# Mixture-of-experts blocks around an attention: the first phase's combines, second half's rows and one activation table stand elsewhere in the order

## The chip, the core and the metric

The kernel runs on one core of a Trainium2 chip. The core has a matrix engine (PE, with its weight loads shown as PEld), a vector engine (DVE), an activation engine (ACT), a general engine (POOL) and a queue engine (SP); each runs its own instructions in the order in which they were written, and they wait for one another on semaphores. The metric is the time of one execution on the device, in microseconds (us), as a median over runs.

## The reference

2048 tokens (4 sequences of 512) of 128 features pass three stages, each on layer-normed input and added to the stream: half of a mixture of 8 experts, a causal attention with one head, half of the same mixture again.

```python
def ffn(x):                       # x: (2048, 128)
    probs = softmax(x @ router_w.T)                  # 8 experts
    topv, topi = top_k(probs, 2)
    topv = topv / (topv.sum(-1) + 1e-9)
    cw = (one_hot(topi, 8) * topv[..., None]).sum(1)
    h = gelu(einsum('td,edh->teh', x, w1))           # h: 512 wide
    y = einsum('teh,ehd->ted', h, w2)
    return einsum('te,ted->td', cw, y)
x = x + 0.5 * ffn(layernorm(x))
x = x + attention(layernorm(x))   # softmax(QK^T / sqrt(128), causal) V
x = x + 0.5 * ffn(layernorm(x))
```

## The kernel before

**Tiling.** A tile is 128 tokens; the tokens are two halves of 8 tiles each. The router sends every token to two experts, and the tokens of one expert are laid into blocks of 128 rows. The first mixture is the *first phase* of 39 blocks, numbered 0 to 38, the attention stands in the middle, and the second mixture is a second phase of 46 blocks. Blocks are grouped into *packs*; the packs of the first phase have 1, 1, 2, 2, 3, 1, 2, 3, 4, 4, 4, 4, 4, 2, 2 blocks, so pack 9 is blocks 19 to 22, pack 11 is blocks 27 to 30, pack 12 is blocks 31 to 34, pack 13 is blocks 35 and 36 and pack 14 is blocks 37 and 38. The first five packs (blocks 0 to 8) hold tokens of the first half alone.

**One block.** POOL gathers its rows by indirect DMA from `xn_rows` in DRAM into `xb_first`. PE transposes a pack's rows (`turn`, L1242), DVE copies the result out of PSUM (`copy_xT`, L986, into `xT_pack`), PE multiplies with the expert's first matrix (`first_product`, L1254), ACT applies Gelu (L589), PE multiplies with the second matrix (`second_product`, L1268), one pack later than the first product, DVE copies the result (`copy_y`, L1006, into `yb_pack`) and SP stores it to `slots_out`. ACT also copies the expert's first matrix into `w1_block` ahead of each block (L583).

**The way back.** `gather(0)` on POOL (L511) fetches, once packs 7 to 9 are stored, the two results of each token of the first half, tile by tile; `gather(1)` does the second half when the last three packs are stored. `combine_and_count` on DVE (L1034, L723, L720) adds two tiles at a time to the stream with their gates and takes the statistics of the layer norm of the attention; there are four such pairs of tiles in a half. `rstd_of` (L738 to L748) turns the statistics into a reciprocal deviation in steps that each wait for the one before, and `normalise_half` (L765) writes `xa`, half a half at a time, which PE transposes (L1187) for the attention's projections (L1308).

**What sets the order.** All orders are written out by hand. Small tables say beside which block (`s` is the block's number plus 2) an engine does a piece of other work: `FIRST_PIECES` routes the second half on DVE and takes the gates, `FIRST_COMBINES` and `FIRST_NORMS` place the combines and the norm, `NUMBERED_BESIDE` places on ACT four copies that fill `numbered`, and `FIRST_FILL` says after which pack's store SP sends them to `slots_in`. A piece of DVE work ends where its generator yields `True`. In DVE's loop, the work beside a block precedes the copy of the next pack's transposes:

```python
for j, c in enumerate(blocks_of(n)):
    beside(c - first + 2)
    if j == turn_at and n + 1 in packs:
        copy_xT(n + 1)
if n > packs[0]:
    copy_y(n - 1)
```

**The start.** DVE takes the statistics of the first half and then runs two chains in turns: the routing of the first half (`route_first`) and `norms`, which is the deviation of the first half, the scaling of the logits, the statistics of the second half, its deviation and `offset_mean`. POOL normalises the first half's rows when the first deviation is there, ACT issues their store to `xn_rows`, and POOL's first gather waits for that store and for the rows' numbers. ACT writes the second half's rows (L560) when `offset_mean` is there, and SP stores them. PE keeps itself busy with throw-away matmuls (L1362): 20 at the start, 8 ahead of the logits, 36 between the routing and block 0.

Of the kernel before, what the change touches and what calls it, by code (L numbers as in the profile page):

```python
# [23 lines left out]
ACT = mybir.ActivationFunctionType  # L24
AX = mybir.AxisListType.X

P = 128
# [7 lines left out]
GT = TILES // GROUPS  # L35
# [19 lines left out]
IDLE_AT_START, IDLE_AT_LOGITS, IDLE_AT_BLOCKS = 20, 8, 36  # L55
# [17 lines left out]
def macaron(nc, x, q_w, k_w, v_w, router_w, w1, w2, out):  # L73
    with ExitStack() as ctx:
        def sb(name, shape, dt=F32):
            return ctx.enter_context(nc.sbuf_tensor(name, shape, dt))
# [45 lines left out]
        offset_mean = sb("offset_mean", [P, GT])  # L122
        xa = [sb(f"xa{g}", [P, GT, D]) for g in range(GROUPS)]
# [153 lines left out]
        NUMBERED_BESIDE = 10, 11, 12, 13  # L277
        NORM_OPS_AHEAD = 6
        FIRST_FILL = 7
        TURN_W_BESIDE, QK_W_BESIDE = 19, 21  # L280
        FIRST_PIECES = (0, 3, 4, 6, 7, 8, 8, 12, 13, 14, 15)
        FIRST_COMBINES = (32, 34, 37)
        FIRST_NORMS = (35, 36, 38, 39)
# [265 lines left out]
        def _(sc):  # L549
# [102 lines left out]
            second_row_tiles()  # L652
            sc.wait_ge(w1_in, 16 * E // 2)

            def soften_second(s):
                if s == 0:
                    exp_logits(1)
                if s in NUMBERED_BESIDE:
                    set_numbered(NUMBERED_BESIDE.index(s))
# [27 lines left out]
        def _(dve):  # L687
# [168 lines left out]
            def place_second():  # L856
# [8 lines left out]
                yield from following(v.tensor_tensor_scan(last_more[:], more[:], more[:], 0.0, ALU.add, ALU.bypass))  # L865
                v.tensor_scalar(seg_end[:, 2 * E:3 * E], last_more[:], seg_end[:, E - 1:E], float(E), ALU.add, ALU.add)
# [107 lines left out]
            def rest(pieces):  # L974
                for _ in pieces:
                    pass
# [129 lines left out]
            norms = chain(rstd_of(0, GT), scale_shifted(0), first_stats(1), rstd_of(GT, GT), scaled_means())  # L1106
# [10 lines left out]
            def beside_first(s):  # L1117
                for _ in range(FIRST_PIECES.count(s)):
                    next_part(pieces)
                if s == TURN_W_BESIDE + 1:  # L1120
                    turned_weights()
                if s == QK_W_BESIDE + 1:
                    scaled_product()
                if s in FIRST_COMBINES:
                    combine_and_count(0, pair_of(FIRST_COMBINES.index(s)))
                if s in FIRST_NORMS:
                    next_part(norm_pieces)
# [3 lines left out]
            rest(norm_pieces)  # L1131
            combine_and_count(0, pair_of(3))
# [308 lines left out]
```

## Time and profile before

| what | us |
|---|---|
| median of 3 runs | 309.33 |
| the runs | 312.15, 309.33, 309.3 |
| the profiled execution | 310.01 |
| its span, first to last instruction | 308.2 |
| busy in the span: PE, DVE, ACT, POOL | 243.1, 138.2, 134.6, 159.5 |

The profile shows one execution, of 310.01 us, of which 308.2 us are between the first and the last instruction. A timeline row gives the start, the length and, in brackets, how long the engine had been idle and what ended that. The granted clock of PE is 1.00 at 2.4 GHz and 0.50 at 1.2 GHz; over the span its mean was 0.875.

### The profile page before, as it was taken

What the parts mean: (1) busy time and instruction counts of PE and PEld (TensorE: products, weight loads), DVE (VectorE), ACT (ScalarE), POOL (GpSimd) and SP (SyncE); (2) the same over time, 40 slices, a digit from 0 to 9 for tenths busy, and PEclk for the clock granted to TensorE, in tenths of its full rate; (3) what the DMA queues carried; (4) which work ended last, traced back from release to release, by engine and by line L of the source; (5) the groups of instructions that cost most, each with busy time, mean ns of one, the idle gap of its engine ahead of it and who ended that gap; (6) DMA issues with size and microseconds to landing.
All of it is one profiled execution on the core that took longest, in us unless ns stands there. A gap on an engine that the chain in (4) does not pass through costs nothing.

```text
span 308.2 us, 5848 instructions
## 1 busy us (share of the span) xinstructions
PE 243.1 (79%) x1930; PEld 226.2 (73%) x1930; DVE 138.2 (45%) x554; ACT 134.6 (44%) x261; POOL 159.5 (52%) x192
## 2 busy tenths in 40 slices
PE   7538999999998894997486915899994999999700
PEld 7537898989998882766354715899994999999700
DVE  4898554422113745589826764243110011343305
ACT  3109529755555112562043514556562456664200
POOL 5627337777247706760715770016777765555740
PEclk9857899999999796897567985979999899999975
DMA  6993113334845322210000114131115324322125
GB/s 190 343 244 111 53 34 98 79 89 140 167 156 183 91 62 53 52 52 0 2 0 26 53 51 103 37 79 35 54 54 155 93 79 126 118 75 65 52 71 168
DMA packets 30509, 28.43 MB, mean 92 GB/s; under 512 B 3513, under 2 KB 25025, under 8 KB 30481
## 3 DMA queue, kind: packets, MB, share of 16 engines
q1 hardware_dynamic: 24656, 17.75, 19.3%
q0 software_dynamic: 4768, 9.79, 12.2%
q10 hardware_dynamic: 1056, 0.53, 0.6%
q8 instruction: 17, 0.28, 0.4%
q14 instruction: 12, 0.09, 0.1%
HBM read 15.23 MB, written 12.82 MB: 91 GB/s over the span
## 4 chain that ended last, share of the span: by engine, by line
PE 51%; DVE 19%; POOL 12%; issue 9%; DMA 5%; ACT 1%; POOLq 1%; DVEq 0%; SPq 0%; ACTq 0%
PE bank L1268 20%; PE bank L1254 19%; POOL slots_in L500 9%; DVE xs L1034 3%; PE bank L1308 2%; PE bank L1242 2%; POOL y_rows L511 2%; PE bank L1311 1%; DVE stats L723 1%; DMA y_rows<-slots_out,slot_of 1%; PE bank L1204 1%; DVE xT_pack L986 1%; POOL final_rows L524 1%; DMA y_rows<-final_rows 1%; PE bank L1187 1%
## 5 line engine op out<-in xcount | busy, mean ns | idle before, releaser
L1254 PE MATMUL bank<-xT_pack,w_block 128*128 128x128 f32 x680 | 95.1, 286 | 6.8 <-DVE xT_pack L986 6.8
L1254 PEld LDWEIGHTS bank<-xT_pack,w_block 128*128 128x128 f32 x680 | 87.1, 201 | 8.4 <-DVE xT_pack L986 8.4
L1268 PE MATMUL bank<-w_sb,act 128*128 x680 | 91.7, 282 | 1.9 <-issue 1.2
L1268 PEld LDWEIGHTS bank<-w_sb,act 128*128 128x128 f32 x680 | 84.9, 198 | 2.7 <-issue 2.7
L589 ACT ACTIVATE act<-bank 128x512 f32<-128x512 f32 x85 | 50.8, 598 | 70.8 <-PE bank L1254 70.7
L583 ACT COPY w_block<-w_sb 128x512 f32 x85 | 51.7, 613 | 13.6 <-issue 13.6
L489 POOL DMA_INDIRECT xb_first<-xn_rows,row_in x39 | 37.1, 952 | 25.4 <-issue 11.3
L511 POOL DMA_INDIRECT y_rows<-slots_out,slot_of x32 | 30.2, 945 | 27.1 <-DMA slots_out<-yb_pack 18.0
L500 POOL DMA_INDIRECT slots_in<-xn_numbered,slot_of x32 | 30.8, 961 | 18.9 <-DVE slot_of L828 9.5
L524 POOL DMA_INDIRECT final_rows<-xb_first,row_of x23 | 22.1, 959 | 31.1 <-DVE xb_first L1006 25.3
L986 DVE COPY xT_pack<-bank 128x512 f32<-128x512 f32 (+3 forms) x29 | 15.9, 547 | 49.3 <-PE bank L1242 44.1
L524 POOL DMA_INDIRECT final_rows<-yb_pack,row_of x23 | 22.4, 973 | 16.9 <-DVE yb_pack L1006 11.7
L1006 DVE COPY yb_pack<-bank 128x512 f32<-128x512 f32 (+3 forms) x22 | 11.7, 530 | 35.4 <-PE bank L1268 33.3
L1034 DVE SCALAR_TENSOR_TENSOR xs<-y_rows,gate,xs 128x128 f32<-128x128 f32 x64 | 18.0, 345 | 18.6 <-DMA y_rows<-slots_out,slot_of 9.8
L477 POOL TENSOR_SCALAR xn_numbered<-xs,moments,rstd 128x128 f32<-128x128 f32 x16 | 12.9, 813 | 17.5 <-DVE rstd L748 17.5
L554 ACT COPY nT<-bank 128x512 f32<-128x512 f32 x12 | 6.8, 585 | 25.7 <-PE bank L1187 25.7
L1242 PE MATMUL bank<-ident,xb_pack 128*128 128x128 f32 x46 | 8.0, 290 | 12.7 <-DMA xb_pack<-slots_in 12.7
L1242 PEld LDWEIGHTS bank<-ident,xb_pack 128*128 128x128 f32 x46 | 6.0, 152 | 13.0 <-issue 9.4
L614 ACT ACTIVATE act<-bank,neg_max 128x128 f32<-128x128 f32 (+3 forms) x16 | 8.4, 526 | 13.1 <-DVE neg_max L1066 13.1
L723 DVE BATCH_NORM_STATS2 stats<-xs 128x6 f32<-128x128 f32 x48 | 13.1, 280 | 1.2 <-DMA xs<-in_L_attn_x 0.7
L1006 DVE COPY xb_first<-bank 128x512 f32<-128x512 f32 (+2 forms) x7 | 4.2, 594 | 21.0 <-PE bank L1268 21.0
L1344 PE MATMUL bank<-act 128*128 128x128 f32 x80 | 12.6, 293 | 0.9 <-ACT act L623 0.9
(170 smaller groups left out, 267.2 us busy)
## 6 DMA issues: line engine op xcount, KB each, us to landing
w_sb<-in_L_ffn_w SPq DMA_DIRECT2D x8, 512.0 KB, 8.6
xb_pack<-slots_in SPq DMA_DIRECT2D x10, 258.0 KB, 3.0
slots_in<-numbered SPq DMA_DIRECT2D x6, 387.0 KB, 4.1
y_rows<-final_rows SPq DMA_DIRECT2D x8, 256.0 KB, 3.8
slots_out<-yb_pack SPq DMA_DIRECT2D x5, 256.0 KB, 2.5
xs<-in_L_attn_x SPq DMA_DIRECT2D x4, 256.0 KB, 3.6
out<-xs SPq DMA_DIRECT2D x8, 128.0 KB, 1.9
slots_in<-numbered SPq DMA_DIRECT2D x2, 322.5 KB, 2.9
```

The lines of the kernel that those rows point to most:

```text
L489: pool.indirect_dma_start(xb_first[:, c, :], None, xn_rows[0:(GT if n < SURE_PACKS else TILES) * P, :], bass.IndirectOffsetOnAxis(ap=row_i ...
L500: pool.indirect_dma_start(slots_in[g], bass.IndirectOffsetOnAxis(ap=slot_of[g][:, k, t:t + 1], axis=0), xn_numbered[g][k][:, t, :], None). ...
L511: pool.indirect_dma_start(y_rows[g][:, t, k, :], None, slots_out[0:(MAX_BLOCKS, SHARED_BLOCKS)[g] * P, :], bass.IndirectOffsetOnAxis(ap=sl ...
L524: pool.indirect_dma_start(final_rows, bass.IndirectOffsetOnAxis(ap=row_of[:, b:b + 1], axis=0), rows, None).then_inc(stored, 16)
L583: nc.scalar.copy(w1_block[c % WIDE_BUFS][:], w1_sb[:, bass.ds(offset(c), H)]).then_inc(w1_copied, 1)
L589: nc.scalar.activation(act[c % WIDE_BUFS][:], h_of(c)[:], ACT.Gelu).then_inc(act_ready, 1)
L723: v.bn_stats(stats[t // GT][:, t % GT, :], xs[:, t, :]).then_inc(counted, 1)
L986: v.tensor_copy(xT_pack[n % 2][:, columns], xT_ps[:, columns]).then_inc(xT_copied, 1)
L1034: add = v.scalar_tensor_tensor(tile, y_rows[g][:, t, k, :], gate[g][:, k, t:t + 1], tile, ALU.mult, ALU.add)
L1242: mm = nc.tensor.transpose(xT_ps[:, j * P:(j + 1) * P], tokens, ident[:])
L1254: mm = nc.tensor.matmul(h_of(c)[:, q * P:(q + 1) * P], w1_block[c % WIDE_BUFS][:, q * P:(q + 1) * P], xT_pack[n % 2][:, j * P:(j + 1) * P] ...
L1268: mm = nc.tensor.matmul(y_ps[n % 2][:, j * D:(j + 1) * D], act[c % WIDE_BUFS][:, q * P:(q + 1) * P], w2_sb[:, bass.ds(at + q * D, D)], sta ...
```

## The change

- On DVE, the combines of the first half stand beside `s` = 36 and 39 instead of 32, 34 and 37; the third pair follows the phase with the fourth. The four pieces of the norm of the first four tiles stand at 39, 39, 40, 40.
- On DVE at the start, the statistics of the second half alternate with the steps of the first half's deviation, ahead of the scaling of the logits, where they stood after it.
- `place_second` yields once more, so that a copy of transposes can come between its steps; `FIRST_PIECES` has one entry more, and the second half's gates stand at 22 and 23.
- On ACT, a Gelu of one column, `gelu_of_one`, stands ahead of the first phase; the softmax's exponential of the second half moves from `s` = 0 to 18.
- The four copies into `numbered` stand at 10, 12, 14, 16, and SP sends them after the stores of packs 8 to 11 instead of 7 to 10. PE starts with 16 throw-away matmuls instead of 20.

```diff
-IDLE_AT_START, IDLE_AT_LOGITS, IDLE_AT_BLOCKS = 20, 8, 36
+IDLE_AT_START, IDLE_AT_LOGITS, IDLE_AT_BLOCKS = 16, 8, 36
...
+        gelu_of_one = sb("gelu_of_one", [P, 1])
...
-        NUMBERED_BESIDE = 10, 11, 12, 13
+        NUMBERED_BESIDE = 10, 12, 14, 16
+        SECOND_EXP_BESIDE = 18
...
-        FIRST_FILL = 7
+        FIRST_FILL = 8
...
-        FIRST_PIECES = (0, 3, 4, 6, 7, 8, 8, 12, 13, 14, 15)
-        FIRST_COMBINES = (32, 34, 37)
-        FIRST_NORMS = (35, 36, 38, 39)
+        FIRST_PIECES = (0, 3, 3, 4, 6, 7, 8, 8, 12, 14, 22, 23)
+        FIRST_COMBINES = (36, 39)
+        FIRST_NORMS = (39, 39, 40, 40)
...
             second_row_tiles()
+            nc.scalar.activation(gelu_of_one[:], ident[:, 0:1], ACT.Gelu)
             sc.wait_ge(w1_in, 16 * E // 2)
...
-                if s == 0:
+                if s == SECOND_EXP_BESIDE:
                     exp_logits(1)
...
                 yield from following(v.tensor_tensor_scan(last_more[:], more[:], more[:], 0.0, ALU.add, ALU.bypass))
+                yield True
...
-            norms = chain(rstd_of(0, GT), scale_shifted(0), first_stats(1), rstd_of(GT, GT), scaled_means())
+            def in_turns(*chains):
+                for _ in zip_longest(*chains):
+                    yield
+
+            norms = chain(in_turns(rstd_of(0, GT), first_stats(1)), scale_shifted(0), rstd_of(GT, GT), scaled_means())
...
-                if s in FIRST_NORMS:
+                for _ in range(FIRST_NORMS.count(s)):
                     next_part(norm_pieces)
...
             rest(norm_pieces)
+            combine_and_count(0, pair_of(2))
             combine_and_count(0, pair_of(3))
```

On DVE at the end of the first phase, from the copy of pack 12's transposes on, there stands before (`xT_pack` takes a pack's transposes, `yb_pack` a pack's results; an `xs<-y_rows0` row of four is one pair of tiles):

```order
L986 COPY xT_pack0<-bank0 128x512
L1034 SCALAR_TENSOR_TENSOR xs<-y_rows0,gate0,xs 128x128 x4
L723 BN_STATS stats0<-xs 128x6 x2
L720 BN_AGGR moments<-stats0 128x2
L1006 COPY yb_pack1<-bank1 128x512
L1034 SCALAR_TENSOR_TENSOR xs<-y_rows0,gate0,xs 128x128 x4
L723 BN_STATS stats0<-xs 128x6
L720 BN_AGGR moments<-stats0 128x2
L723 BN_STATS stats0<-xs 128x6
L720 BN_AGGR moments<-stats0 128x2
L986 COPY xT_pack1<-bank0 128x256
```

and after:

```order
L990 COPY xT_pack0<-bank0 128x512
L1010 COPY yb_pack1<-bank1 128x512
L990 COPY xT_pack1<-bank0 128x256
L1038 SCALAR_TENSOR_TENSOR xs<-y_rows0,gate0,xs 128x128 x4
L726 BN_STATS stats0<-xs 128x6 x2
L723 BN_AGGR moments<-stats0 128x2
L1010 COPY yb_pack2<-bank4 128x512
L990 COPY xT_pack0<-bank0 128x256
L1010 COPY yb_pack0<-bank1 128x512
L1038 SCALAR_TENSOR_TENSOR xs<-y_rows0,gate0,xs 128x128 x4
```

The first two combines stood ahead of the copies of pack 10's results and of pack 13's transposes; now the first stands behind both, and the second behind pack 12's results.

On DVE a little later, from the first four tiles' `xa` to the rest of the half, there stands before:

```order
L765 TENSOR_SCALAR xa0<-xs,moments,rstd 128x128 x4
L1006 COPY yb_pack1<-bank4 128x256
L1006 COPY yb_pack2<-bank1 128x256
L1034 SCALAR_TENSOR_TENSOR xs<-y_rows0,gate0,xs 128x128 x4
L723 BN_STATS stats0<-xs 128x6
L720 BN_AGGR moments<-stats0 128x2
```

and after, where one pair more follows the phase's last copies:

```order
L768 TENSOR_SCALAR xa0<-xs,moments,rstd 128x128 x4
L1010 COPY yb_pack1<-bank4 128x256
L1010 COPY yb_pack2<-bank1 128x256
L1038 SCALAR_TENSOR_TENSOR xs<-y_rows0,gate0,xs 128x128 x4
L726 BN_STATS stats0<-xs 128x6 x2
L723 BN_AGGR moments<-stats0 128x2
L1038 SCALAR_TENSOR_TENSOR xs<-y_rows0,gate0,xs 128x128 x4
```

On DVE in the routing of the second half (`place_second`), around the copy of block 1's transpose, there stands before:

```order
L865 SCALAR_TENSOR_TENSOR last_more<-more 128x8
L866 TENSOR_SCALAR seg_end<-last_more,seg_end 128x8
L867 TENSOR_TENSOR first_block<-last_more,more 128x8
L868 SCALAR_TENSOR_TENSOR shift<-first_block,rev_e 128x8
L986 COPY xT_pack1<-bank0 128x128
L870 TENSOR_TENSOR beyond<-beyond,shift 128x64
```

and after, with the copy three operations earlier:

```order
L868 SCALAR_TENSOR_TENSOR last_more<-more 128x8
L990 COPY xT_pack1<-bank0 128x128
L870 TENSOR_SCALAR seg_end<-last_more,seg_end 128x8
L871 TENSOR_TENSOR first_block<-last_more,more 128x8
L872 SCALAR_TENSOR_TENSOR shift<-first_block,rev_e 128x8
L874 TENSOR_TENSOR beyond<-beyond,shift 128x64
```

On ACT around the Gelu of block 17 (`act1` here; `w1_block4` is block 20's matrix) there stands before:

```order
L589 ACTIVATE act0<-bank2 128x512
L583 ISA
L583 COPY w1_block4<-w1_sb 128x512
L589 ACTIVATE act1<-bank3 128x512
L336 TENSOR_LOAD expert_at
L338 ISA
L583 COPY w1_block5<-w1_sb 128x512
```

and after, with the second half's exponential and two table loads between:

```order
L591 ACTIVATE act0<-bank2 128x512
L585 ISA
L585 COPY w1_block4<-w1_sb 128x512
L573 ACT_TABLE_LOAD
L573 ACTIVATE expd1<-shifted1 128x64
L591 ACT_TABLE_LOAD
L591 ACTIVATE act1<-bank3 128x512
```

## Rows read from the trace of the kernel before

**Rows 1.** Page, part 4: chain that ended last, shares of the span.

```profile
PE 51%; DVE 19%; POOL 12%; issue 9%; DMA 5%; ACT 1%; POOLq 1%; DVEq 0%; SPq 0%; ACTq 0%
```

**Rows 2.** Timeline of PE, end of the first phase (start, length, what, idle).

```profile
97.80 1.06 PE L1268 MATMUL bank<-w_sb,act 128*128 x8
...
101.53 2.08 PE L1254 MATMUL bank<-xT_pack,w_block 128*128 128x128 f32 x8 [2.67 <-DVE xT_pack L986]
103.40 1.74 PE L1268 MATMUL bank<-w_sb,act 128*128 x8
...
111.45 2.85 PE L1268 MATMUL bank<-w_sb,act 128*128 x24
...
119.72 1.09 PE L1187 MATMUL bank<-ident,xa 128*128 128x128 f32 x4 [4.26 <-DVE xa L765]
```

**Rows 3.** Timeline of DVE over the same stretch.

```profile
93.78 0.88 DVE L1034 SCALAR_TENSOR_TENSOR xs<-y_rows,gate,xs 128x128 f32<-128x128 f32 x3 [1.49 <-DMA y_rows<-slots_out,slot_of]
...
99.75 0.88 DVE L1034 SCALAR_TENSOR_TENSOR xs<-y_rows,gate,xs 128x128 f32<-128x128 f32 x3 [3.12 <-DMA y_rows<-slots_out,slot_of]
...
101.08 0.39 DVE L986 COPY xT_pack<-bank 128x256 f32<-128x256 f32 x1
...
108.97 0.69 DVE L1006 COPY yb_pack<-bank 128x512 f32<-128x512 f32 x1 [2.20 <-PE bank L1268]
...
114.33 0.42 DVE L1006 COPY yb_pack<-bank 128x256 f32<-128x256 f32 x1 [1.31 <-PE bank L1268]
114.67 1.13 DVE L1034 SCALAR_TENSOR_TENSOR xs<-y_rows,gate,xs 128x128 f32<-128x128 f32 x4
...
116.52 0.17 DVE L738 TENSOR_SCALAR var_eps<-moments 128x4 f32<-128x4 f32 x1
...
119.01 1.14 DVE L765 TENSOR_SCALAR xa<-xs,moments,rstd 128x128 f32<-128x128 f32 x4
```

**Rows 4.** 1 us stretch: PE, PEld, DVE, ACT, POOL busy; clock; DMA.

```profile
102.00:103.00 1.00, 1.00 (x7) 1.00 (x7) 0.83 (x6) 0.00 (x0) 0.70 (x2) 0.50 0.16 41
```

**Rows 5.** Timeline of POOL at the start: normalised rows, first gather.

```profile
10.74 6.39 POOL L477 TENSOR_SCALAR xn_numbered<-xs,moments,rstd 128x128 f32<-128x128 f32 x8 [5.97 <-DVE rstd L748]
23.49 1.19 POOL L489 DMA_INDIRECT xb_first<-xn_rows,row_in  x1 [6.36 <-DMA xn_rows<-xn_numbered]
```

**Rows 6.** Page, part 5: all 48 statistics of the layer norms.

```profile
L723 DVE BATCH_NORM_STATS2 stats<-xs 128x6 f32<-128x128 f32 x48 | 13.1, 280 | 1.2 <-DMA xs<-in_L_attn_x 0.7
```

**Rows 7.** Timeline of DVE, routing of the first and the second half.

```profile
19.30 2.35 DVE L888 TENSOR_TENSOR at_row<-col_no,slot_row 128x1024 f16<-128x1024 f32 x2
...
28.42 0.17 DVE L865 TENSOR_TENSOR_SCAN last_more<-more 128x8 f32<-128x8 f32 x1
...
29.16 0.29 DVE L986 COPY xT_pack<-bank 128x128 f32<-128x128 f32 x1
```

**Rows 8.** Timeline of PE, keep-busy matmuls and the first blocks.

```profile
22.16 4.00 PE L1362 MATMUL bank<-ones 128*128 128x128 bf16 x36
26.43 0.30 PE L1242 MATMUL bank<-ident,xb_first 128*128 128x128 f32 x1 [0.26 <-DMA xb_first<-xn_rows,row_in]
...
27.26 1.14 PE L1254 MATMUL bank<-xT_pack,w_block 128*128 128x128 f32 x8
...
29.51 1.90 PE L1254 MATMUL bank<-xT_pack,w_block 128*128 128x128 f32 x8 [1.01 <-DVE xT_pack L986]
```

**Rows 9.** Stretch of 1 us at the first blocks, columns as above.

```profile
30.00:31.00 1.00, 1.00 (x7) 1.00 (x7) 0.64 (x3) 0.94 (x2) 0.99 (x1) 0.50 0.29 74
```

**Rows 10.** DMA issues, median us to landing; landings of those issued at 26:27.

```profile
xb_first<-xn_rows,row_in POOLq DMA_INDIRECT x39, 2.7
...
DMA to landing us min/median/max: 3.8/3.8/3.9
```

**Rows 11.** Timeline of ACT: table of Gelu, and Gelu of block 17.

```profile
28.54 1.28 ACT L589 ACT_TABLE_LOAD   x1
...
65.41 0.60 ACT L589 ACTIVATE act<-bank 128x512 f32<-128x512 f32 x1 [2.00 <-PE bank L1254]
```


## The prediction

> **What bounds the kernel now.** I read the chain that ended last first: PE holds half of it, DVE a fifth, POOL an eighth, ACT a hundredth [rows 1]. So an ACT edit pays only where PE or DVE waits for ACT, and a DVE edit where PE waits for DVE. Then the timelines of PE and DVE, at the two places that the change touches.
>
> At the end of the first phase PE stops once: after the product that ends at 98.86 (97.80 + 1.06) it is idle for 2.67 us, released by DVE's copy of pack 13's transposes [rows 2]. DVE was late because it stood in its second combine, which waited 3.12 us for tile 3 of `gather(0)` until 99.75; only then came the copy, at 101.08 [rows 3]. After the stall PE was granted half its clock (0.50, the 1.2 GHz level) [rows 4], and the next two products took 2.08 and 1.74 us instead of 1.06 [rows 2]: another 1.70 us. So the early combine costs PE 2.67 + 1.70 = 4.37 us.
>
> When the phase ends for PE (111.45 + 2.85 = 114.30), DVE still has the last copy, one combine and a deviation, and PE waits 4.26 us for `xa` [rows 2, 3]. From there the attention follows, and all later work hangs on it.
>
> At the start, POOL's first gather is released by the store of the normalised rows, at 23.49, not by the rows' numbers [rows 5]. Block 0's turn follows its landing by little (26.43, after 0.26 idle), and first products run at 27.26 and 29.51, the second after 1.01 us of waiting for DVE [rows 8]. That second one took 1.90 us, at half clock [rows 8, 9].
>
> **The combines moved (the main term).** The first pair's data was there by 93.78 [rows 3]; beside `s` = 36 DVE reaches it after copying pack 13's transposes, so that a wait there would hold up only pack 11's results. The second pair, there by 99.75, is reached after pack 12's results, 5 us later. So neither wait reaches PE any more. PE then ends its phase 4.37 us earlier, at 109.9, and pack 12's results come at 108.97 - 4.37 = 104.6.
>
> What DVE does from there decides what is kept. A combine of two tiles with statistics takes 1.6 us: 1.33 from 99.75 to 101.08 for three of its four adds, and 0.28 for the fourth (1.13 / 4) [rows 3]; with the last statistics it is 1.85 (114.67 to 116.52). The deviation takes 2.49 us (116.52 to 119.01), `xa` of four tiles 1.14 [rows 3]. So after the change: copy of pack 12's results, 104.6 to 105.3 (0.69); second combine to 106.9; deviation to 109.4; `xa` to 110.5; two late copies of 0.42 to 111.4. That is 1.5 us behind PE's end, where before it was 0.45. Then the third combine, new behind the phase, to 113.0, and the old tail of 4.34 us (114.67 to 119.01) to 117.3. `xa` thus starts 1.7 us earlier than at 119.01. With 1.85 for each of the two combines it is 1.3; with pieces that overlap better, 2.1. I take **1.8 of the 4.37 us** as kept: the rest is given back on DVE. `gather(1)` needs the last pack's store, which comes 3 us earlier, so it is not next in line.
>
> **The statistics moved.** Eight statistics of 0.28 us [rows 6] go out of the turns with routing, where each delayed a chain step, into the wait for the first logits. The second deviation's small steps take their places, so `at_row`, which ended at 21.65 [rows 7], ends up to 8 x 0.28 = 2.2 us earlier, at least 1; I take 1.7. On the path this is worth nothing: POOL's gather waits for the rows' store. That store hangs on the first deviation, which now shares its turns with the last two statistics: 0 to 0.5 us later, I take 0.2.
>
> It does move two things. The 36 keep-busy matmuls follow the routing and so start near 20.5 instead of 22.16, and their 4.00 us [rows 8] end near 24.5, where block 0's turn comes at 26.6: a hole of 2 us where there were 0.26. And the second half's rows are written on ACT some 5 us earlier, so their store no longer meets the gathers of blocks 2 and 3. A gather beside it took 3.8 to 3.9 us to land, the median is 2.7 [rows 10]; now it is mostly over when the first gather starts. Both bounds are 0 and 1.2 us; I take 0.
>
> **The break in `place_second`.** Block 1's transposes can be copied after the scan (28.42 + 0.17 = 28.6) instead of at 29.16 [rows 7]: 0.55 us for PE, which waits just there [rows 8].
>
> **The clock at the start.** In this execution a half-clock stretch fell on two products, block 1's first and block 0's second, for about 0.85 us each (1.90 - 1.06). With the hole, such a stretch may fall earlier, on block 0, where part of the time goes to waiting anyway, or come twice. From 1.7 us won (none left) to 1.7 lost (two); I take 0.35 won. The Trainium skill (TensorE: Matmul & The Clock Gate, Part 1) says that idle PE time takes the clock back to half, and that the gate runs on its own time, not from a kernel's start, so that the place of a change varies from run to run. That speaks against a hole ahead of block 0, and for ends on both sides; rows 4 and 9 agree with the first, no run here shows the second. By the first alone the start would be the third case below.
>
> So the start gives 0.55 - 0.2 + 0.35 = **0.7 us**, from -1.1 to 2.1.
>
> **ACT's tables.** Gelu's table load of 1.28 us [rows 11] goes ahead of block 0. Before, Gelu of block 0 ended about 30.4 (28.54 + 1.28 + 0.60), and its reader on PE stood behind a product that ended at 31.41 (29.51 + 1.90) [rows 8]: worth nothing. The second half's exponential now needs two loads beside block 17: 2 x 1.28 + 0.25 = 2.8 us, of which 2.00 lie in an idle spell [rows 11]. Gelu of block 17 comes 0.8 us late. Its bank is next needed by block 21's first product, four blocks or some 7 us on (two products of nearly 1 us each, and turns), and the gates on DVE that read the exponential stand at `s` = 22. Worth nothing, with about 4 us of cover.
>
> The Trainium skill (ScalarE: Activation LUTs, What ACT_TABLE_LOAD costs) puts a switch at 2.66 us with a drain, and its rule is to do all of one set before the next, which speaks against this edit. The row of the load shows 1.28 us [rows 11]. By the page the two switches would be 5.6 us, 3.6 late, still inside the cover; so the sum is the same, and the page only adds chance to the slower end.
>
> **The rest, at nothing.** Four throw-away matmuls fewer (4 x 0.11 us at 4.00 / 36 each [rows 8]) end ahead of transposes that wait for the tokens. The `numbered` copies and fills are needed only after the attention; the fill after pack 11's store now lies beside `gather(0)`, whose later tiles are read 5 us after they land.
>
> **The sum.** 1.8 + 0.7 = 2.5 us. The profiled execution was 310.01 us, of which 308.2 span; it would become 307.5. The median of the runs lies 0.7 lower, so the forecast is 309.33 - 2.5 = **306.8 us**.
>
> **Rivals.**
> 1. *The half-clock stretch falls into the hole and the early blocks run at full clock.* The start gives 2.1, the end 1.8: 305.4. For it: the wait of 1.01 us ahead of block 1's product, with which the stretch came [rows 8], is halved. Against: the hole is new idle time just ahead of the blocks.
> 2. *The hole costs a second half-clock stretch*: the start loses 1.1, the end gives 1.8: 308.6.
> 3. *The change doesn't do what it says at the end*: the wait moves from PE to DVE's tail in full, since one combine and two late copies follow the phase. The end gives 0.2, the start 0.5: 308.6.
> 4. *Slower.* The hole leaves PE at half clock over blocks 0 to 3, eight products instead of two: six more at 0.85 is 5.1 us, against 0.55 - 0.2 + 1.8 = 2.15 won: 312.3. It turns slower from three further products at half clock. Against: in rows 8 and 9 the stretch covered two products, and PE is busy from block 1 on.
>
> **How the numbers follow.** Chances: forecast 0.53 (305.7 to 307.9), rival 1 0.20, rival 2 0.11, rival 3 0.09, rival 4 0.07. The range runs from a little below rival 1 to 309.4, past rivals 2 and 3: 304.9 to 309.4. One per cent, about what a measurement of this kernel can tell from no change, is 3.1 us: faster means below 306.2. That is rival 1 and the lower quarter of the forecast, 0.35; slower by over 1% (above 312.4) is half of rival 4 and what I have not seen, 0.05; the rest is 0.60.
>
> **What would show it.** Right: PE has no idle piece over 1 us between block 2 and the end of the phase; DVE's combines wait for no gather; the two last result copies run some 1 us after PE's end; `xa` of the second four tiles starts 5 us or more after PE's last product, and 1.5 to 3.5 us earlier than at 119.01. At the start, the keep-busy matmuls end 1.5 us or more ahead of block 0's turn, and POOL's first gather is again released by the rows' store, near 23.5. On ACT, two table loads before block 17's Gelu, and no PE wait for ACT near block 21. Wrong: a PE wait for `xT_pack` still at pack 13 or 14, products of 1.9 us at block 4 or later, or an attention that starts no earlier although PE's phase ended earlier.

## The result, and the profile after

The changed kernel takes **306.52 us** (median of 20 runs, 305.14 to 309.14), the kernel before on the same chip 309.51 (20 runs, 305.68 to 312.15). The ratio is 0.9935, 95% interval 0.9905 to 0.9964: 2.0 us less (1.1 to 2.9). The two medians alone differ by more, 3.0 us; gains are given below by the ratio, with its interval where it matters. The forecast was 306.8 us, 2.5 less. On a second chip (e5_changed_again) the ratio was 0.9949 [0.9906, 0.9992], 1.6 us less. The profiled execution took 306.71 us, 304.9 of them span (310.01 and 308.2 before).

Lines after the change are numbered anew: the first product is L1263, the second L1277, the turn L1251, the copy of transposes L990, that of results L1010, the combine L1038, `xa` L768.

Timeline of PE at the end of the first phase, after the change (start, length, what, idle before it):

```profile
105.77 2.84 PE L1277 MATMUL bank<-w_sb,act 128*128 x24
110.09 0.66 PE L1196 MATMUL bank<-ident,xa 128*128 128x128 f32 x4 [1.47 <-DVE yb_pack L1010]
116.43 1.09 PE L1196 MATMUL bank<-ident,xa 128*128 128x128 f32 x4 [5.68 <-DVE xa L768]
```

There is no stall at pack 13 any more [rows 2], and PE's phase ends at 105.77 + 2.84 = 108.61 instead of 114.30. But PE then waits twice, 1.47 us for a late result copy and 5.68 us for `xa`. Before, the second wait was 4.26 us [rows 2] and the first 0.52:

```profile
114.81 0.66 PE L1187 MATMUL bank<-ident,xa 128*128 128x128 f32 x4 [0.52 <-DVE yb_pack L1006]
```

DVE's timeline over the same stretch, after the change, shows what PE waits for:

```profile
92.30 1.13 DVE L1038 SCALAR_TENSOR_TENSOR xs<-y_rows,gate,xs 128x128 f32<-128x128 f32 x4
...
103.29 0.69 DVE L1010 COPY yb_pack<-bank 128x512 f32<-128x512 f32 x1 [2.81 <-PE bank L1277]
103.90 1.13 DVE L1038 SCALAR_TENSOR_TENSOR xs<-y_rows,gate,xs 128x128 f32<-128x128 f32 x4
...
108.13 1.11 DVE L768 TENSOR_SCALAR xa<-xs,moments,rstd 128x128 f32<-128x128 f32 x4
109.28 0.76 DVE L1010 COPY yb_pack<-bank 128x256 f32<-128x256 f32 x2
109.95 1.13 DVE L1038 SCALAR_TENSOR_TENSOR xs<-y_rows,gate,xs 128x128 f32<-128x128 f32 x4
...
111.47 1.10 DVE L1038 SCALAR_TENSOR_TENSOR xs<-y_rows,gate,xs 128x128 f32<-128x128 f32 x4
...
115.74 1.12 DVE L768 TENSOR_SCALAR xa<-xs,moments,rstd 128x128 f32<-128x128 f32 x4
```

No combine waits for a gather (no bracket), as intended [rows 3]. DVE is idle for 3.25, 2.21 and 2.81 us in turn ahead of its copies at 97.16, 100.05 and 103.29, and then has the second combine, a whole deviation, `xa` of the first four tiles, both last result copies, the third and the fourth combine and the second deviation in one unbroken row from 103.29 to 115.74. `xa` starts 3.27 us earlier than before.

The start, on PE (the keep-busy matmuls, block 0's turn, block 1's first and block 0's second product), to be read against [rows 8]:

```profile
21.86 4.00 PE L1371 MATMUL bank<-ones 128*128 128x128 bf16 x36
26.09 0.34 PE L1251 MATMUL bank<-ident,xb_first 128*128 128x128 f32 x1 [0.23 <-DMA xb_first<-xn_rows,row_in]
...
28.53 1.16 PE L1263 MATMUL bank<-xT_pack,w_block 128*128 128x128 f32 x8 [0.45 <-DVE xT_pack L990]
30.55 1.15 PE L1277 MATMUL bank<-w_sb,act 128*128 x8 [0.41 <-ACT act L591]
```

The keep-busy matmuls begin 0.3 us earlier and end 0.23 us ahead of block 0's turn: the hole that I had announced isn't there. Block 1's product waits 0.45 instead of 1.01 us and runs in 1.16 instead of 1.90. Stretches of 1 us (busy PE, PEld, DVE, ACT, POOL; granted clock; DMA) at the two places where the clock had been 0.50 [rows 4, 9]:

```profile
30.00:31.00 1.00, 0.59 (x6) 0.45 (x5) 0.59 (x3) 0.83 (x2) 0.69 (x2) 1.00 0.24 66
102.00:103.00 1.00, 1.00 (x12) 1.00 (x11) 0.00 (x0) 0.00 (x0) 0.73 (x1) 1.00 0.68 231
112.00:113.00 1.00, 0.00 (x0) 0.00 (x0) 1.00 (x7) 0.00 (x0) 0.20 (x1) 0.50 0.00 0
```

The first two are at 1.00 now. The third lies in PE's wait for `xa`, and a stretch of half clock lies there in the kernel before too:

```profile
120.00:121.00 1.00, 1.00 (x5) 0.93 (x4) 0.15 (x1) 0.15 (x1) 0.78 (x1) 0.50 0.26 66
```

By such 1 us stretches it runs from about 118.5 to 125.3 before and from 111.5 to 121.8 after, so in the longer wait it begins earlier. It has not moved there from pack 13.

Three points divide the span: block 0's turn, the first product of pack 3 (35.18 after the change, 36.89 before; it waits 0.57 us for its copy in both) and `xa` of the second four tiles. Up to the turn the profile after is 0.34 us ahead, which is not the change's: e1, whose start is that of before, has the same 26.09. From there to pack 3 it is 1.37 us ahead, from pack 3 to `xa` 1.56, behind it nothing. All runs, in us (from the timelines; "stall" is PE's wait at pack 13):

| profiled run | turn | to pack 3 | to xa | to the end | block 1's product: wait, length | stall |
|---|---|---|---|---|---|---|
| before | 26.43 | 10.46 | 82.12 | 189.2 | 1.01, 1.90 | 2.67, half clock behind it |
| before again (e8) | 26.16 | 10.55 | 82.16 | 189.3 | 1.01, 2.08 | 3.63, half clock |
| changed | 26.09 | 9.09 | 80.56 | 189.2 | 0.45, 1.16 | none |
| changed again (e5) | 26.64 | 9.14 | 80.82 | 191.6 | 0.45, 1.16 | none |
| combines only (e1) | 26.09 | 9.66 | 80.14 | 188.6 | 1.00, 1.16 | none |
| start only (e2) | 28.17 | 9.22 | 79.88 | 189.7 | 0.46, 1.16 | 2.77, full clock |
| start only (e11) | 27.74 | 9.03 | 79.59 | 187.7 | 0.45, 1.16 | 2.38, full clock |
| break only (e3) | 26.73 | 9.77 | 82.91 | 189.8 | 0.46, 1.16 | 3.85, half clock |
| statistics only (e6) | 26.71 | 9.19 | 82.71 | 189.2 | 0.84, 1.16 | 3.56, half clock |
| combines between (e4) | 27.90 | 9.08 | 78.02 | 188.6 | 0.45, 1.16 | none |
| the same (e9) | 26.29 | 9.16 | 78.24 | 188.4 | 0.45, 1.16 | none |
| third combine inside (e12) | 26.52 | 9.08 | 79.65 | 188.2 | 0.45, 1.16 | none |

The profiled executions of e7 and e10 are among the longest of their kernels and stand outside the table.

### The profile page after: what moved, and what is told of

Same layout as the page of the kernel before. It is cut to its first block, busy times and chain, and to the rows that moved or that the text cites. A ratio compares the mean times of both kernels' runs of the same rounds, so it can differ in the third digit from the quotient of the medians.

```text
span 304.9 us, 5844 instructions
## 1 busy us (share of the span) xinstructions
PE 237.8 (78%) x1926; PEld 220.1 (72%) x1926; DVE 138.5 (45%) x554; ACT 136.9 (45%) x264; POOL 159.7 (52%) x192
## 4 chain that ended last, share of the span: by engine, by line
PE 51%; DVE 16%; POOL 12%; issue 9%; DMA 8%; ACT 1%; SPq 1%; POOLq 0%; DVEq 0%; ACTq 0%
PE bank L1277 21%; PE bank L1263 20%; POOL slots_in L502 9%; DVE xs L1038 3%; PE bank L1251 2%; PE bank L1317 2%; POOL xn_numbered L479 2%; DMA xn_rows<-xn_numbered 2%; DMA xs<-in_L_attn_x 2%; DMA y_rows<-final_rows 1%; DVE stats L726 1%; PE bank L1320 1%; DVE xa L768 1%; POOL final_rows L526 1%; DVE xT_pack L990 1%
## 5 line engine op out<-in xcount | busy, mean ns | idle before, releaser
L1263 PE MATMUL bank<-xT_pack,w_block 128*128 128x128 f32 x680 | 93.3, 282 | 3.5 <-DVE xT_pack L990 3.5
L1277 PE MATMUL bank<-w_sb,act 128*128 x680 | 90.8, 280 | 2.4 <-issue 1.7
L1263 PEld LDWEIGHTS bank<-xT_pack,w_block 128*128 128x128 f32 x680 | 85.6, 198 | 5.0 <-DVE xT_pack L990 5.0
L1277 PEld LDWEIGHTS bank<-w_sb,act 128*128 128x128 f32 x680 | 83.5, 195 | 4.0 <-issue 3.9
L990 DVE COPY xT_pack<-bank 128x512 f32<-128x512 f32 (+3 forms) x29 | 15.9, 548 | 54.3 <-PE bank L1251 49.1
L1010 DVE COPY yb_pack<-bank 128x512 f32<-128x512 f32 (+3 forms) x22 | 11.6, 531 | 38.9 <-PE bank L1277 38.7
L1038 DVE SCALAR_TENSOR_TENSOR xs<-y_rows,gate,xs 128x128 f32<-128x128 f32 x64 | 17.9, 345 | 8.7 <-DMA y_rows<-final_rows 8.7
L1251 PE MATMUL bank<-ident,xb_pack 128*128 128x128 f32 x46 | 7.8, 285 | 12.5 <-DMA xb_pack<-slots_in 12.5
L1251 PEld LDWEIGHTS bank<-ident,xb_pack 128*128 128x128 f32 x46 | 5.8, 149 | 12.9 <-issue 9.4
L1010 DVE COPY xb_first<-bank 128x512 f32<-128x512 f32 (+2 forms) x7 | 4.2, 594 | 21.1 <-PE bank L1277 21.1
```

The lines of the kernel that those rows point to most:

```text
L990: v.tensor_copy(xT_pack[n % 2][:, columns], xT_ps[:, columns]).then_inc(xT_copied, 1)
L1038: add = v.scalar_tensor_tensor(tile, y_rows[g][:, t, k, :], gate[g][:, k, t:t + 1], tile, ALU.mult, ALU.add)
L1251: mm = nc.tensor.transpose(xT_ps[:, j * P:(j + 1) * P], tokens, ident[:])
L1263: mm = nc.tensor.matmul(h_of(c)[:, q * P:(q + 1) * P], w1_block[c % WIDE_BUFS][:, q * P:(q + 1) * P], xT_pack[n % 2][:, j * P:(j + 1) * P] ...
L1277: mm = nc.tensor.matmul(y_ps[n % 2][:, j * D:(j + 1) * D], act[c % WIDE_BUFS][:, q * P:(q + 1) * P], w2_sb[:, bass.ds(at + q * D, D)], sta ...
```

## The experiments

**My theory** after the result was that the moved combines give what the forecast says, limited by DVE's tail, and that half-clock stretches come by chance. **The rival**: the start's edits give most of it.

**e1_combines_only.** The kernel before with the moved combines alone:

```diff
-FIRST_COMBINES = (32, 34, 37)
-FIRST_NORMS = (35, 36, 38, 39)
+FIRST_COMBINES = (36, 39)
+FIRST_NORMS = (39, 39, 40, 40)
 rest(norm_pieces)
+combine_and_count(0, pair_of(2))
```

> The kernel before with the combines and the norm's pieces placed as in the changed kernel, and nothing else. Theory A (the end gives what DVE's tail leaves of PE's 4.4 us): no wait of PE at pack 13, PE's last product some 4 us earlier (near 110.3 in a profile whose start is as before), xa of the second four tiles 1.6 us earlier, the time 1.3 to 2.1 us below the kernel before. Theory B (rival 3, the wait only moves into DVE's tail and the whole gain is the start's): the time within 0.5 us of the kernel before.

Measured: 307.4 us, 0.9929 [0.9888, 0.9969] of the kernel before (310.66 in that set of four): 2.2 us less (1.0 to 3.5), as much as the whole change. That is a little above theory A's 1.3 to 2.1; theory B falls. On PE:

```profile
29.05 1.16 PE L1255 MATMUL bank<-xT_pack,w_block 128*128 128x128 f32 x8 [1.00 <-DVE xT_pack L986]
...
116.57 1.09 PE L1188 MATMUL bank<-ident,xa 128*128 128x128 f32 x4 [5.72 <-DVE xa L765]
```

The wait for `xa` is the changed kernel's (5.72). Block 1's product waits as before, yet runs at full clock: this part of the code was not edited, so the stretch of [rows 9] does not belong to the code alone.

**e2_start_only and e11_start_again.** The changed kernel with the combines where they were:

```diff
-FIRST_COMBINES = (36, 39)
-FIRST_NORMS = (39, 39, 40, 40)
+FIRST_COMBINES = (32, 34, 37)
+FIRST_NORMS = (35, 36, 38, 39)
 rest(norm_pieces)
-combine_and_count(0, pair_of(2))
```

> The changed kernel with the combines and the norm's pieces placed as before: the start, tables and fills of the change alone. Theory A: PE's wait at pack 13 is back (2 to 3 us, released by DVE), and the time is 0.4 to 1.7 us below the kernel before. Theory B: the whole gain of 2 to 3 us is here. Theory C (the start's gain in the profile was only the place of one half-clock stretch): no difference that can be measured, within 0.5 us.

> All edits of the start and none of the combines, as in e2_start_only, timed in more runs. If the three edits add as they were measured alone: 0 to 1.5 us under the kernel before, with the stall of 2.7 to 3.9 us at pack 13 and the half-clock stretch behind it, as in three other kernels that kept the early combine. Rival, that e2_start_only's 3.7 us was of the kernel: again 3 us or more under the kernel before, and again no half-clock stretch behind the stall.

Measured: 307.24, 0.988 [0.9828, 0.9933] (6 runs), and 307.18, 0.9962 [0.9917, 1.0006] (12 runs): 3.7 (2.1 to 5.3) and 1.2 us less (-0.2 to 2.6). The second set is about what the start's edits give one by one below (0.6, 0.5 and 0), and no more than the first theory allowed; the first set is more. The stall is there; what follows it is not what I expected (e11, PE):

```profile
100.47 1.16 PE L1262 MATMUL bank<-xT_pack,w_block 128*128 128x128 f32 x8 [2.38 <-DVE xT_pack L990]
101.47 1.06 PE L1276 MATMUL bank<-w_sb,act 128*128 x8
```

Both run at full clock at once, in both profiles (1.16 us is what a product takes there after a wait). The kernel before, the break alone and the statistics alone all went to half clock here.

**e3_break_only.**

```diff
-FIRST_PIECES = (0, 3, 4, 6, 7, 8, 8, 12, 13, 14, 15)
+FIRST_PIECES = (0, 3, 3, 4, 6, 7, 8, 8, 12, 13, 14, 15)
 yield from following(v.tensor_tensor_scan(last_more[:], ...))
+yield True
```

> The kernel before with only the one more break in place_second and its place in FIRST_PIECES, so that block 1's transposes are copied before three small operations. Theory A: PE's wait ahead of block 1's first product falls from 1.0 to 0.4 us, the time falls by about 0.5 us, more where the half-clock stretch at the first blocks goes away with it (up to 1.7 us). If the statistics' order is what moved the start, nothing is seen here and PE's first two products keep 1.9 us.

Measured: 309.36, 0.9981 [0.9943, 1.002]: 0.6 us, not to be told from none. On PE:

```profile
29.34 1.16 PE L1255 MATMUL bank<-xT_pack,w_block 128*128 128x128 f32 x8 [0.46 <-DVE xT_pack L987]
31.04 0.44 PE L1243 MATMUL bank<-ident,xb_first 128*128 128x128 f32 x2 [0.54 <-DMA xb_first<-xn_rows,row_in]
```

The wait shrinks by 0.55 us as forecast, and 0.54 us, nearly all of it, comes back at block 2's turn, which now waits for its gather. In the changed kernel this second wait is gone: the second half's rows are stored early, and the gathers of these blocks land in 2.6 us instead of 3.9.

**e6_statistics_only.**

```diff
-norms = chain(rstd_of(0, GT), scale_shifted(0), first_stats(1), ...)
+norms = chain(in_turns(rstd_of(0, GT), first_stats(1)), scale_shifted(0), ...)
```

> The kernel before, with only the second half's statistics put in turn with the first deviation's steps. My forecast's step says: at_row about 1.7 us (at least 1) earlier than 21.65, and 0 in the time (at most 0.2 slower), since POOL's gather waits for the store of the rows. After the changed kernel's trace I expect instead that at_row ends only some 0.3 us earlier, and the second half's rows are written some 4 us earlier. Rival, that this part carries the start's gain: 1.5 to 3.5 us faster, with the gathers of blocks 2 and 3 landing in 2.7 instead of 3.8 us and block 2's turn not waiting.

Measured: 309.17, 0.9985 [0.9948, 1.0021]: 0.5 us, not to be told from none. `at_row` ends 0.1 us earlier (DVE, e6):

```profile
19.19 2.36 DVE L888 TENSOR_TENSOR at_row<-col_no,slot_row 128x1024 f16<-128x1024 f32 x2
```

The second half's rows are written from 18.69 on instead of 23.12. The rival's time does not come, though the gathers of blocks 2 and 3 land as it says, in 2.5 to 2.7 us.

**e7_tables_as_before.** The changed kernel with both table edits undone:

```diff
-nc.scalar.activation(gelu_of_one[:], ident[:, 0:1], ACT.Gelu)
-SECOND_EXP_BESIDE = 18
+SECOND_EXP_BESIDE = 0
```

> The changed kernel without Gelu's table ahead of block 0, and with the second half's exponential ahead of block 0 again. If the tables are worth nothing, as my forecast says: the time of e5_changed_again within 1 us, and Gelu of block 0 about 1.3 us later with no PE wait behind it over 0.5 us. Rival, that the early table is on the path now that block 0's and 1's products run at full clock: PE waits some 0.7 to 1.3 us for ACT ahead of block 0's second product, and the time is 1 us above e5_changed_again.

Measured: 307.61, against 307.83 for e5_changed_again on the same chip; both ratios are 0.9949. Gelu's table stands between the weights' copies again (ACT, e7), and PE waits 0.41 us ahead of block 0's second product in e7 as in the changed kernel. The rival falls. ACT, then PE, in e7:

```profile
30.12 1.28 ACT L591 ACT_TABLE_LOAD   x1
31.41 0.60 ACT L591 ACTIVATE act<-bank 128x512 f32<-128x512 f32 x1
```

```profile
32.91 1.15 PE L1276 MATMUL bank<-w_sb,act 128*128 x8 [0.41 <-issue]
```

**e5_changed_again and e8_before_again.** Both kernels as they are.

> The changed kernel once more, on the chip of the next three runs. If the two parts add (2.2 and 3.7 us in the runs of each alone), it is 5 to 6 us faster than the kernel before. If they don't add, it is 2 to 3.5 us faster, as in its first measurement, and then one part's gain has no place left beside the other's. In its profile, if the half-clock stretches at the first blocks are chance: block 1's first product at either 1.16 or about 1.9 us, whichever; if the change took them away: 1.16 again, and a granted clock of 1.0 from the keep-busy matmuls on.

> The kernel before once more, for a second profile of it. If the half-clock stretches at block 1's first product and behind pack 13's stall belong to the kernel: both again, products of about 1.9 and 2.1 us at the same two places. If they are chance of the execution: at least one of them is elsewhere or gone, while PE's waits for xT_pack (1.01 and 2.67 us) stand where they were within 0.6 us.

Measured: e5 307.83, 1.6 us less (0.2 to 2.9). So the parts don't add: 2.2 and 1.2 to 3.7 alone, 1.6 to 2.0 together. The profile of e8, PE:

```profile
29.34 2.08 PE L1254 MATMUL bank<-xT_pack,w_block 128*128 128x128 f32 x8 [1.01 <-DVE xT_pack L986]
...
101.57 2.07 PE L1254 MATMUL bank<-xT_pack,w_block 128*128 128x128 f32 x8 [3.63 <-DVE xT_pack L986]
103.43 1.55 PE L1268 MATMUL bank<-w_sb,act 128*128 x8
```

The same stalls, the second 0.96 us longer than in the first profile, followed by half clock at the same two places [rows 2, 8]. "Chance of the execution" is too simple: it is a thing that this kernel tends to.

**e4_between and e9_between_again.** The changed kernel, with no combine behind the phase but the last:

```diff
-FIRST_COMBINES = (36, 39)
-FIRST_NORMS = (39, 39, 40, 40)
+FIRST_COMBINES = (36, 38, 39)
+FIRST_NORMS = (38, 38, 40, 40)
 rest(norm_pieces)
-combine_and_count(0, pair_of(2))
```

> The changed kernel with the second combine and half of the norm one step earlier, ahead of the copy of pack 14's transposes, where DVE idles 3.25 and 2.21 us, and with the third combine ahead of pack 13's results instead of behind the phase. Theory A (DVE's tail is what binds): xa of the second four tiles starts 1.5 to 2.5 us earlier than in the changed kernel, and the time is 1.5 to 2.5 us below it, 304 to 305. Its rival: the attention's start hangs on something else (the clock after the pause, the gather of the second half), and nothing is gained; or DVE then holds up pack 14's transposes, PE waits over 0.5 us for them, and less than 1 us is gained.

> The changed kernel with its first three combines beside s = 36, 38 and 39 and none of them behind the phase, as in e4_between, timed in more runs. If DVE's tail is what takes back the gain of the combines: PE waits 4.2 us for xa (the changed kernel 5.7), and the time is 4 to 6.5 us under the kernel before, 2 to 3.5 under the changed kernel. Rival, that the six runs of e4_between fell on favourable clock stretches: 2 to 3 us under the kernel before, the changed kernel's own gain.

Measured: 304.17, 0.9808 [0.9763, 0.9854], and 304.31, 0.9857 [0.9802, 0.9911]: 6.0 and 4.4 us less than the kernel before. These two sets are the fastest here; both first theories hold. DVE and then PE in e9:

```profile
97.98 1.13 DVE L1038 SCALAR_TENSOR_TENSOR xs<-y_rows,gate,xs 128x128 f32<-128x128 f32 x4
...
104.29 1.13 DVE L1038 SCALAR_TENSOR_TENSOR xs<-y_rows,gate,xs 128x128 f32<-128x128 f32 x4
...
106.37 1.12 DVE L768 TENSOR_SCALAR xa<-xs,moments,rstd 128x128 f32<-128x128 f32 x4
...
109.39 1.13 DVE L1038 SCALAR_TENSOR_TENSOR xs<-y_rows,gate,xs 128x128 f32<-128x128 f32 x4
...
113.69 1.14 DVE L768 TENSOR_SCALAR xa<-xs,moments,rstd 128x128 f32<-128x128 f32 x4
```

```profile
109.53 0.65 PE L1195 MATMUL bank<-ident,xa 128*128 128x128 f32 x4 [0.52 <-DVE yb_pack L1010]
114.40 1.09 PE L1195 MATMUL bank<-ident,xa 128*128 128x128 f32 x4 [4.22 <-DVE xa L768]
```

The second combine is ready at 97.98 without a wait, the deviation runs in time in which DVE was idle, and only one combine is left behind the phase: PE waits 0.52 and 4.22 us instead of 1.47 and 5.68, 2.41 less. From pack 3 to `xa` it is 78.24 (e4: 78.02) instead of 80.56.

**e10_between_alone.** The kernel before with the combines of e9 and nothing of the start.

> The kernel before with the combines as in e9_between_again, and nothing of the start. If the start's edits are worth little (0 to 1 us, as e3_break_only, e6_statistics_only and e7_tables_as_before say one by one): 3.5 to 5.5 us under the kernel before, within 1 us of e9_between_again. Rival, that they are worth the 3.7 us of e2_start_only: 1 to 2.5 us under the kernel before, and 3 us or more above e9_between_again.

Measured: 305.79, 0.9883 [0.9835, 0.993], 3.6 us less; the first theory's number. From pack 3 to `xa` its profile has 78.39 us, as e4 and e9 have with the start's edits. The start adds 0.8 us by the ratios, which is inside their intervals.

**e12_third_combine_inside.** As e9, but `FIRST_NORMS = (39, 39, 40, 40)` as in the changed kernel.

> The changed kernel with its combines beside s = 36, 38 and 39 and none behind the phase, but the deviation's steps where the change has them (beside 39 and 40). It tells the third combine's place from the deviation's. If the 1.5 us of the combine behind the phase is all: PE's wait for xa 4.2 to 4.5 us, xa within 0.5 us of e9_between_again, and its time. Rival, that the deviation of 2.5 us and xa of 1.1 us, still ahead of the last two copies, hold DVE's tail as well: xa 0.8 to 1.5 us later than e9_between_again, between it and the changed kernel.

Measured: 304.89, 0.9876 [0.9818, 0.9935]; in time not to be told from e9. PE:

```profile
111.23 0.66 PE L1195 MATMUL bank<-ident,xa 128*128 128x128 f32 x4 [1.47 <-DVE yb_pack L1010]
115.74 1.19 PE L1195 MATMUL bank<-ident,xa 128*128 128x128 f32 x4 [3.85 <-DVE xa L768]
```

From pack 3 to `xa` it is 79.65, which is 0.9 under the changed kernel and 1.4 over e9: the rival. The late deviation and the first `xa` ahead of the last two copies hold DVE's tail as well (PE's 1.47 us for the copy stay).

## Why the prediction was right, and where it was not

**The combines moved (1.8 of 4.37).** Right in mechanism, and in size against the kernel before. The two profiles of the changed kernel are 1.6 and 1.3 us shorter from pack 3 to `xa`, e1 2.0; the bounds were 1.3 to 2.1. On PE the stall's end gave 3.98 us from pack 3 on (from 87.87 to 82.52 us between block 0's turn and the phase's end, less the start's 1.37), 0.4 under my 4.37. Of that, 0.14 is in the half-clock term: I set the two slow products against 1.06 each, but at full clock a product takes 1.16 after a wait (e11). By the start of pack 14's turn, 4.34 us behind the stalled product's start before and 2.78 in both start-only profiles, the half clock cost 1.56 us and not 1.70. The rest I did not trace. And from PE's end to `xa` it is 7.13 us instead of 4.71, so DVE gave back 2.42, where my sum had 2.57. e9, e10 and e12 show that it is DVE's tail: work taken out of it comes off the stretch to `xa`, and in e4 clearly off the time (a ratio of 0.9763 to 0.9854, the changed kernel 0.9905 to 0.9964; the intervals of e9, e10 and e12 touch the changed kernel's).

What I had not weighed is that half of the 4.37 is not the wait itself. The stall alone is 2.4 to 2.8 us in the start-only kernels, about what DVE's tail takes back; the rest, 1.4 to 1.6 us by the start of pack 14's turn (before, e8, e3, e6), is half-clock products behind it. In the start-only profiles these don't follow, and there the stretch from pack 3 to `xa` is even shorter (79.9 and 79.6) than in the changed kernel (80.6 and 80.8): against them the move loses 0.7 to 1.2 us. That accounts for a good part of why the parts don't add. The other part is that the stall itself ends 0.7 to 1.6 us sooner behind pack 3 in the start-only profiles (63.99 and 63.70 us) than in those four (64.64 to 65.34); why, is open, and no run has the moved fills alone. Whether the start's edits themselves keep the clock up, or the two profiled executions of that kernel happened to, is open too: both are among those with long first logits (last section), and none of the four with half clock behind the stall is.

**The statistics moved (worth 0).** The 0 held, the step under it failed: "`at_row` ends 1.7 us earlier (at least 1)", and with it the hole ahead of block 0. It ended 0.29 us earlier. The chain's `over` on DVE before:

```profile
13.38 0.23 DVE L835 TENSOR_TENSOR over<-bank,block_end 128x64 f32<-128x64 f32 x1 [0.53 <-PE bank L1217]
```

and DVE in the changed kernel:

```profile
13.55 0.22 DVE L838 TENSOR_TENSOR over<-bank,block_end 128x64 f32<-128x64 f32 x1 [0.42 <-PE bank L1226]
...
19.00 2.36 DVE L892 TENSOR_TENSOR at_row<-col_no,slot_row 128x1024 f16<-128x1024 f32 x2
...
27.98 0.17 DVE L868 TENSOR_TENSOR_SCAN last_more<-more 128x8 f32<-128x8 f32 x1
28.18 0.29 DVE L990 COPY xT_pack<-bank 128x128 f32<-128x128 f32 x1
```

I had taken all eight statistics off the routing's chain. In the timeline of before only four of them lie between the chain's `over` (13.38) and `at_row` (19.30); the others stand ahead of it, one of them in its wait for PE. From `over` to `at_row` the chain is now 5.45 us instead of 5.92, and it starts 0.17 later since the two last statistics stand among the logits' steps. Deviation steps that took their turns cost 0.15 to 0.4 each. So there was no hole, and rivals 1, 2 and 4, which needed one, were never put to the test. That the early blocks ran at full clock is as rival 1 has it, but without its hole.

The 0.2 for a later first deviation cannot be told from chance: POOL starts on the rows 0.29 us later, as forecast, but kernels with that code unedited start between 10.37 (e1) and 11.10 (e3), and the wait for their store was 5.77 instead of 6.36 us, so that the gather came 0.30 earlier. POOL in the changed kernel, to be read against [rows 5]:

```profile
11.03 6.39 POOL L479 TENSOR_SCALAR xn_numbered<-xs,moments,rstd 128x128 f32<-128x128 f32 x8 [6.26 <-DVE rstd L751]
23.19 1.19 POOL L491 DMA_INDIRECT xb_first<-xn_rows,row_in  x1 [5.77 <-DMA xn_rows<-xn_numbered]
```

**The break (0.55)** was right to 0.01 for the wait (0.45 instead of 1.01 us; the copy at 28.18 follows the scan at 27.98), but not for the path. Alone it gives nearly all of that back to the gather of block 2, which my 0 for the early store of the rows had missed: 0.54 us (e3; of the 3.8 and 3.9 us in [rows 10] the gather's is 3.9, the other is the store's). Among profiles with no half clock at the first blocks, the way from the turn to pack 3 is 9.66 us with the start of before (e1), 9.77 with the break, 9.19 with the statistics and 9.03 to 9.22 with both. So the two together are worth some 0.5 us there, and one profile of each says that the statistics, at 0 in my sum, bring most of it.

**The clock at the start (0.35)** was too low for the execution: both half-clock products ran at full clock (0.74 and 0.64 us less), and the way to pack 3 became 1.37 shorter, with 0.41 of new waiting for ACT ahead of block 0's second product. As a mean it may be right. Over the profiles, with e7 and e10, the stretch followed a wait of 1.0 us in three of four (not in e1), 0.84 us in none of one, and 0.45 us in none of nine; that points to the shorter wait, but e3, with the break alone, timed only 0.6 us (-0.6 to 1.8) less. Not settled. The Trainium skill (TensorE: Matmul & The Clock Gate, Part 1) says that the gate runs on its own time; e1 against e8, the same instructions up to block 1 with and without the stretch, agrees with it.

**ACT's tables (0).** Right. The changed kernel's ACT:

```profile
21.70 1.28 ACT L655 ACT_TABLE_LOAD   x1
...
61.80 1.28 ACT L573 ACT_TABLE_LOAD   x1
...
63.37 1.28 ACT L591 ACT_TABLE_LOAD   x1
64.66 0.60 ACT L591 ACTIVATE act<-bank 128x512 f32<-128x512 f32 x1
```

Two loads of 1.28 us beside block 17, no wait of PE behind them, and e7 without them takes the same time. Gelu starts right behind its load (63.37 + 1.28 = 64.65), so a switch is 1.28 us in this kernel. The higher price that the prediction quoted from the Trainium skill is not seen. Another page of the Trainium skill (ScalarE activation tables: per-element evaluation and per-set limits, What a function is on this engine) has 1283 ns, which the rows bear out.

**The signs.** `xa` 3.27 us earlier (1.5 to 3.5), 7.13 us behind PE's end (5 or more), no pause of PE over 1 us in the phase, POOL's first gather again released by the rows' store, at 23.19: as written. The keep-busy matmuls 1.5 us ahead of the turn: not so.

**Rival 3**, the wait that moves into DVE's tail in full, came true by a good half: 2.42 of 4.37.

**The sum.** The start's 0.7 came out near the 0.8 of e9 against e10, in part by luck: the hole did not come, the break's 0.55 was not won on the path by the break, and the clock's 0.35 is unsettled. Its lower end was also added up wrongly (0.55 - 0.2 - 1.7 is -1.35, not -1.1), which moves rival 2 by 0.25 us. And the two terms were added as if each were sure; the runs give 2.2 for the combines alone, 1.2 to 3.7 for the start alone and 1.6 to 2.0 for both.

**Sorted by clock.** Each run has its mean granted clock. Among the 66 runs of the kernel before in the three sets of experiments, the 14 at 0.874 to 0.877 have a median of 310.95 us, the 16 at 0.884 to 0.895 of 308.3. At 0.883 to 0.895 the others are: break only 308.5 (6 runs), combines only 306.65 (5), start only 306.6 (7), changed 306.35 (10), e10 305.3 (6), e4 and e9 303.9 (9). Runs recorded above that (eight of the kernel before, with a median of 312.3) are left out: all five profiles with long first logits lie there, at 0.90 to 0.92, and the last section shows that their record is wrong at the start. This sorts runs after the fact and is no experiment. But it suggests that stretches of half clock are worth some 2.6 us between executions of one kernel, that either part of the change alone reaches what both reach, and that the way to gain more is the one of e9.

## What to carry to other kernels

When a stall is removed from the engine that bounds, add up what the engine behind it still has to do after the last block: what is moved behind the end of a phase is paid there, and a place inside the phase where the data is ready and the engine idle (e9) is worth more than one that is merely safe (the changed kernel). Count a half-clock stretch behind a stall as a term of its own with a chance, not as a part of the stall. And when operations leave a chain, count those between its last wait and its result, not all of them.

## What the hardware showed that I had not expected

The 16 matmuls of the first half's logits take 1.90 us in seven profiled executions (2.08 and 2.23 in e5 and e12) and 3.53 in five, with the granted clock recorded as 1.00 in all; here the changed kernel and e4, PE:

```profile
6.12 1.90 PE L1213 MATMUL bank<-router_T,nT 128*128 128x8 f32 x16
```

```profile
6.49 3.53 PE L1212 MATMUL bank<-router_T,nT 128*128 128x8 f32 x16
```

The second half's logits, at a recorded 0.50 in the changed kernel, take 3.56:

```profile
13.38 3.56 PE L1213 MATMUL bank<-router_T,nT 128*128 128x8 f32 x16
```

In the five executions they take the same 3.56 at a recorded 1.00. So the long ones ran at the lower level, which the record doesn't show, and block 0's turn came at 27.7 to 28.4 us in those five profiles (e2, e4, e7, e10, e11) and at 26.1 to 26.7 in all others, whatever the kernel. That is 1.6 us between executions, nearly as much as the change is worth.
